# K's bias as a row added on VectorE, n3 made on ScalarE, and a new order of the opening, in a one-core transformer block

## The chip, the cores and the metric

The kernel runs on one core of a Trainium2 chip. The metric is the device time of one execution in microseconds (us). Below, PE is TensorE, DVE is VectorE, ACT is ScalarE, POOL is GpSimd and SP is SyncE, whose queue issues DMAs.

## The reference

There are 16 sequences of 256 tokens with 128 features, all in float32. Cut to what matters:

```python
sa, ca, ga, sb, cb, gb = modulation(silu(c) @ wmod)        # per sequence, gates clipped away from 0
h = layernorm(x) * (1 + ca) + sa
# attention layer with 16 heads of 8, softmax-free
Q = elu(h @ Wq + bq) + 1
K = elu(h @ Wk + bk) + 1
V = h @ Wv + bv
KV, Ksum = einsum(K, V), K.sum(tokens)
att = Q @ KV / (Q @ Ksum + 1e-6)                           # per head
x1 = layernorm(h + att @ Wo + bo) * g1 + beta1
z  = x1 + relu(x1 @ W1 + b1) @ W2 + b2                     # hidden width 512
x  = x + ga * (layernorm(z) * g2 + beta2)                  # x2 in the kernel
h2 = layernorm(x) * (1 + cb) + sb                          # n3 is this layernorm
xr, xk = token mixes of h2 and h2 one token before
out = x + gb * sigmoid(xr @ W_r) * (relu(xk @ W_k) ** 2 @ W_v)
```

## The kernel before, in words

Each engine runs a program that is written out by hand, and engines meet through semaphores alone: `need(engine, signal, count)` is a wait in front of the next instruction of that engine. An engine never passes a waiting instruction. A sequence is two chunks of 128 tokens (NC = 2).

The work is a pipeline over sequences. Step t starts sequence t (n1, K, Q, the state), and at the same time does the attention of sequence t-1, the feed-forward part of t-2, the second residual x2 and the norm n3 of t-3, and the mixing layer of t-4. Steps 0 to 2 are written out as `first_steps`. Steps 3 to 15 have a fixed order on each engine, and from step 4 on all parts are present, so that there are 12 full steps, 4 to 15. Step 16 drains, and a hand-written end finishes the last sequences.

What matters for one full step t, with the names used later:

- PE, in `step`: transposes of n1 (t), the attention product, transposes of ny (t-2), transposes of n3 (t-4), `k_product` (a bias product of line 1203 and four records of line 1206), `q_product`, three of four hidden products, attention transposes, the last hidden product, `state_product` (line 1222, it needs `k_ok`), `output_product`, then `mix_products`: line 1190, the key product of t-4, needs `mixk_ok`, the K half of the tile mixT, and line 1194, the receptance product, needs `mix_ok`, the R half. The feed-forward products of line 1140 end the step and raise `z_mm`.
- DVE, in `step`: it begins with `step_end`, whose statistics of z wait for `z_mm` of the step before. Then come the product with the tanh, the mean and variance of z, statistics of the next x, denominators and reciprocals, `centred`, `attention`, `k_elu`, `middle` (x2), the statistics of x2, and the two instructions of `mix_half`, K first. Later come the statistics of y, `q_elu`, the two instructions of `take_n3`, which wait for POOL's rstd of n3, `masked_state` and `y_norm`.
- ACT: hT and x1T out of the transposes, keepT, the exponents for K and Q, the hidden layer's relu, the state, and at the step's end tanh and n1 of the next sequence.
- POOL: each norm's power -0.5, and sums that need no PSUM.

K's bias in the kernel before is a product in bf16: the bias row is split into bf16 parts (`bias_part`), which stand in three rows of `bias_parts`, and each `k_product` multiplies them with `ones3` into bank 4 before the product with hT is added. exp_k and k_elu both read bank 4.

The first n1 is made from rstd and a shift: POOL multiplies mean and rstd (`mean_r`), subtracts (`shift_n1`), and then ACT takes chunk 0 and DVE chunk 1.

## Time and profile before

| what | value |
|---|---|
| median of 3 runs | 163.57 us (163.56 to 163.71) |
| the profiled execution | 162.83 us, its span 161.0 us |
| PE busy | 156.1 us, 97% of the span, granted clock full in all 40 slices |
| DVE busy | 128.8 us, 80% |
| ACT busy | 116.9 us, 73% |
| POOL busy | 105.1 us, 65% |
| chain that ended last | PE 88%, DVE 5%, POOL 2%, issue 2%, ACT 1% |

The span is the time on the core from the first to the last instruction. Busy time counts an engine's own instructions. In the chain each moment is given to the instruction for which the last one, followed back, had to wait.

### The profile page before, as it was taken

The page shows a single profiled execution, that of the slowest core. Times are in us where ns is not written, and L with a number is a line of the kernel's source. Part 1 is how long each engine was busy: PE and PEld are TensorE (multiplying, and loading weights), DVE is VectorE, ACT ScalarE, POOL GpSimd, SP SyncE. Part 2 cuts the span into 40 slices and gives each one's busy share as a digit, 9 for nine tenths or more (in the row PEclk, how much of TensorE's full clock was granted, in tenths as well). Part 3 has the DMA queues.
Part 4 walks back from the last instruction along what each step waited for, and adds up shares of the span by engine and source line. Part 5 has one row for each costly group of instructions (what it writes and reads, how often), then busy time and mean ns, then how long its engine had stood idle before and what let it go on. Part 6 is the DMA issues. An engine that isn't in the chain of part 4 may idle for free.

```text
span 161.0 us, 4072 instructions
## 1 busy us (share of the span) xinstructions
PE 156.1 (97%) x1151; PEld 145.8 (91%) x1151; DVE 128.8 (80%) x585; ACT 116.9 (73%) x320; POOL 105.1 (65%) x243
## 2 busy tenths in 40 slices
PE   7999999999999999999999999999999999999992
PEld 6878898999999999999999999999999999898891
DVE  3866878698888979797988888897979878887842
ACT  4256776789695969696987959595969787556562
POOL 4337567476676767787676767676777755972631
PEclk9999999999999999999999999999999999999999
DMA  4925279940010101010100101010101000010112
GB/s 124 255 100 160 80 215 338 429 199 0 2 33 4 33 0 33 4 35 2 33 5 0 33 6 33 0 33 4 33 2 35 4 4 28 2 37 2 33 29 69
DMA packets 8973, 9.93 MB, mean 62 GB/s; under 512 B 724, under 2 KB 7416, under 8 KB 8952
## 3 DMA queue, kind: packets, MB, share of 16 engines
q1 hardware_dynamic: 8656, 9.60, 19.1%
q8 instruction: 9, 0.15, 0.4%
q10 hardware_dynamic: 296, 0.08, 0.2%
q14 instruction: 12, 0.10, 0.2%
HBM read 7.55 MB, written 2.13 MB: 60 GB/s over the span
## 4 chain that ended last, share of the span: by engine, by line
PE 88%; DVE 5%; issue 2%; POOL 2%; ACT 1%; DVEq 0%; POOLq 0%
PE bank L1140 16%; PE bank L1250 15%; PE bank L1129 8%; PE bank L1222 5%; PE bank L1206 4%; PE bank L1178 4%; PE bank L1214 4%; PE bank L1166 4%; PE bank L1134 4%; PE bank L1362 3%; PE bank L1194 3%; PE bank L1190 3%; PE bank L1233 3%; PE bank L1070 2%; PE bank L1203 1%
## 5 line engine op out<-in xcount | busy, mean ns | idle before, releaser
L1140 PE MATMUL bank<-w,hid 128*128 128x128 f32 x240 | 31.7, 275 | 0.0
L1250 PE MATMUL bank<-x1T,w 128*128 128x256 f32 x120 | 30.9, 381 | 0.0
L1140 PEld LDWEIGHTS bank<-w,hid 128*128 128x128 f32 x240 | 29.3, 192 | 0.0
L347 ACT ACTIVATE hid<-bank,b_cols 128x256 f32<-128x256 f32 x60 | 26.0, 511 | 1.1 <-PE bank L1250 1.1
L534 POOL TENSOR_TENSOR rstd_n<-vare_n,power 128x2 f32<-128x2 f32 x30 | 23.8, 792 | 2.4
L323 ACT ACTIVATE hT<-bank,modT 128x256 f32<-128x256 f32 x16 | 9.0, 564 | 20.8 <-PE bank L1129 20.7
L1250 PEld LDWEIGHTS bank<-x1T,w 128*128 128x128 f32 x120 | 21.5, 190 | 2.6 <-ACT x1T L328 0.2
L530 POOL TENSOR_TENSOR vare_n<-mv_n,eps 128x2 f32<-128x2 f32 x30 | 5.8, 194 | 17.3 <-DVE mv_n L694 17.2
L292 ACT ACTIVATE n<-x_all,shift_n,rstd_n 128x128 f32<-128x128 f32 x27 | 11.8, 485 | 2.5 <-POOL shift_n L542 2.5
L700 DVE TENSOR_SCALAR ny<-bank,mv_ny,rstd_ny 128x128 f32<-128x128 f32 x32 | 11.6, 405 | 2.5 <-POOL rstd_ny L534 1.2
L700 DVE TENSOR_SCALAR n<-x,mv_n,rstd_n 128x128 f32<-128x128 f32 x28 | 8.4, 343 | 6.0 <-POOL rstd_n L534 6.0
L317 ACT ACTIVATE keepT<-bank,modT 128x255 f32<-128x255 f32 x26 | 13.1, 555 | 0.0
L534 POOL TENSOR_TENSOR rstd_ny<-vare_ny,power 128x2 f32<-128x2 f32 x16 | 11.9, 746 | 1.3
L588 POOL TENSOR_TENSOR out_sb<-x,prod 128x256 f32<-128x256 f32 x15 | 10.9, 726 | 2.8 <-DVE x L797 1.2
L685 DVE BATCH_NORM_STATS2 stats_z<-bank 128x6 f32<-128x128 f32 x30 | 7.4, 289 | 6.0 <-PE bank L1140 5.9
L1129 PE MATMUL bank<-ident,n 128*128 128x128 f32 x62 | 11.9, 273 | 0.0
L530 POOL TENSOR_TENSOR vare_z<-mv_z,eps 128x2 f32<-128x2 f32 x14 | 2.7, 195 | 13.7 <-DVE mv_z L694 13.7
L1166 PE MATMUL bank<-kqvo,attT 128*128 128x128 f32 x64 | 11.5, 275 | 0.0
L581 POOL TENSOR_TENSOR xb<-x_all,gm_rows 128x256 f32<-128x256 f32 x15 | 10.9, 724 | 0.8 <-DVE x L797 0.8
L822 DVE SCALAR_TENSOR_TENSOR mixT<-bank,modT,keepT 128x256 f32<-128x256 f32 x26 | 11.2, 470 | 0.0
L328 ACT ACTIVATE x1T<-bank,beta_b,cols 128x256 f32<-128x256 f32 x15 | 8.5, 563 | 3.7 <-PE bank L1129 2.5
L1178 PE MATMUL bank<-kvs,qT 128*128 128x144 f32 x64 | 10.7, 289 | 0.0
(186 smaller groups left out, 454.1 us busy)
## 6 DMA issues: line engine op xcount, KB each, us to landing
gm_rows<-mod_rows_dram SPq DMA_DIRECT2D x2, 960.0 KB, 9.6
out<-out_sb SPq DMA_DIRECT2D x15, 128.0 KB, 1.8
gm_rows<-mod_rows_dram SPq DMA_DIRECT2D x1, 768.0 KB, 6.8
w<-in_w SPq DMA_DIRECT2D x1, 512.0 KB, 5.5
x_all<-in_x SPq DMA_DIRECT2D x1, 512.0 KB, 5.5
bv_row<-bv_rows_dram SPq DMA_DIRECT2D x1, 512.0 KB, 7.7
bv_row<-bv_rows_dram SPq DMA_DIRECT2D x1, 384.0 KB, 4.3
gm_rows<-mod_rows_dram SPq DMA_DIRECT2D x1, 384.0 KB, 4.1
```

The source lines that it names most:

```text
L292: last = nc.scalar.activation(n1[s % 2][:, c, :], x_all[:, NC * s + c, :], ACT.Identity, scale=rstd["n1"][:, c:c + 1], bias=shift_n1[:, c: ...
L317: nc.scalar.activation(keepT[:, i, 1:L], banks[2][:, 0:L - 1], ACT.Identity, scale=mod_col(KEEP + i, s), bias=mod_col(SB, s)).then_inc((ke ...
L347: last = nc.scalar.activation(hid[:, f, :], bank[:, f % 2 * L:(f % 2 + 1) * L], ACT.Relu, bias=b1_cols[:, f:f + 1])
L534: nc.gpsimd.tensor_tensor(rstd[name][:, :], vare[name][:, :], power[:, :], ALU.pow).then_inc(rstd_ok[name], 1)
L581: nc.gpsimd.tensor_tensor(tile[:, :, :], x_all[:, NC * s:NC * (s + 1), :], gm_rows[:, s, GB_ROW:GB_ROW + 1, :].broadcast_to([128, NC, D]), ...
L700: last = nc.vector.tensor_scalar(dest[:, c, :], source(c), mv[name][:, c, 0:1], rstd[name][:, c:c + 1], ALU.subtract, ALU.mult)
L822: nc.vector.scalar_tensor_tensor(mixT[:, i, :], banks[2][:, 0:L], modT[:, MOVE + i, s:s + 1], keepT[:, i, :], ALU.mult, ALU.add).then_inc( ...
L1129: last = nc.tensor.transpose(bank[:, c * 128:(c + 1) * 128], tile[:, c, :], ident[:, :])
L1140: last = nc.tensor.matmul(banks[6][:, c * D:(c + 1) * D], hid[:, f, c * 128:(c + 1) * 128], w2[:, f, :], start=False, stop=(f == FF - 1 an ...
L1166: last = nc.tensor.matmul(banks[1][:, c * D:(c + 1) * D], attT[:, c * 128:(c + 1) * 128], wo, start=False, stop=(c == NC - 1))
L1178: last = nc.tensor.matmul(attention_bank(s)[:, c * (D + H):(c + 1) * (D + H)], qT[:, c * 128:(c + 1) * 128], kvs[:, :], start=True, stop=True)
L1250: return nc.tensor.matmul(bank[:, f % 2 * L:(f % 2 + 1) * L], w1[:, f * 128:(f + 1) * 128], x1T[:, :], start=True, stop=True)
```

## The change

Three things are changed together.

1. K's bias. Only sequence 0 still gets it by a product, now one float32 product of `ones_row` and `bias_rows`. For the others `k_product` has no bias product. DVE adds the bias row to bank 4 in a new instruction, `k_biased`, which writes kb, and exp_k and k_elu read kb. The casts and splits of `bias_part` are gone, and bk is loaded into 128 partitions instead of 3.
2. n3 in steps 3 to 15. The two instructions of `take_n3` leave DVE. DVE makes a small shift (`shift_of_n3`), and ACT makes n3 after n1 at its step's end. `centred` and the statistics of the next x change places in DVE's step.
3. The opening. The first n1 is made by DVE alone, both chunks, from mean and rstd as in the other norms, into the tile n1[1], and it is transposed from there. ACT makes n1[0] for the state product besides. Two warming products are gone, and `direct_row`, `direct_weights` and others come later.

```diff
             def k_exponent(s):
-                need(act, k_mm, s + 1)
-                nc.scalar.activation(exp_k[:, :, :], chunked(banks[4]), ACT.Exp, bias=neg1[:, :]).then_inc(expk_ok, 1)
+                if s == 0:
+                    act.wait_ge(k_mm, 1)
+                need(act, kb_ok, s)
+                source = kb[:, :, :] if s else chunked(banks[4])
+                nc.scalar.activation(exp_k[:, :, :], source, ACT.Exp, bias=neg1[:, :]).then_inc(expk_ok, 1)
...
+                if live(t):
+                    take_n3(t - 3)
+            def take_n3(s):
+                need(act, shift_ok, s + 1)
+                need(act, h2T_mm, s)
+                for c in range(NC):
+                    last = nc.scalar.activation(n3[:, c, :], x2[s % 3][:, c, :], ACT.Identity, scale=rstd["n3"][:, c:c + 1],
+                                                bias=shift_n3[:, c:c + 1])
+                last.then_inc(n3_ok, 1)
...
-            bias_part(0)
-            n1_chunk(0, 1).then_inc(n1_half, 1)
+            normalise("n1", n1[1], x_chunk(0), 1, n1_turn)
...
+            def shift_of_n3(s):
+                need(dve, rstd_ok["n3"], s + 1)
+                need(dve, n3_ok, min(s, LAST - 2))
+                nc.vector.scalar_tensor_tensor(shift_n3[:, :], mv["n3"][:, :, 0], -1.0, rstd["n3"][:, :], ALU.mult,
+                                               ALU.mult).then_inc(shift_ok, 1)
...
+            def k_biased(s):
+                need(dve, k_mm, s + 1)
+                need(dve, bias_rows_ok, 1)
+                nc.vector.tensor_tensor(kb[:, :, :], chunked(banks[4]), bias_rows[:, :].unsqueeze(1).broadcast_to([128, NC, D]),
+                                        ALU.add).then_inc(kb_ok, 1)
...
             def k_product(s):
+                if s == 0:
+                    pe.wait_ge(const_dve, 6)
+                    pe.wait_ge(bias_rows_ok, 1)
+                    nc.tensor.matmul(chunked(banks[4]), ones_row[:, :], bias_rows[:, :].unsqueeze(1).broadcast_to([128, NC, D]),
+                                     start=True, stop=False)
...
-                nc.tensor.matmul(chunked(banks[4]), ones3[:, :], bias_parts[:, :].unsqueeze(1).broadcast_to([128, NC, D]),
-                                 start=True, stop=False)
```

In a full step of DVE, from the mean and variance of z to the mixing, this stands in the kernel before (z is the centred z1, att the attention, x_2 the second residual, mixT the two mixing halves):

```order
L694 BN_AGGR mv_z<-stats_z 128x2 x2
L685 BN_STATS stats_n<-x_all 128x6 x2
L841 TENSOR_SCALAR den<-bank 128x32
L694 BN_AGGR mv_n<-stats_n 128x2 x2
L845 RECIPROCAL rden<-den 128x32
L787 SCALAR_TENSOR_TENSOR z<-bank,mv_z,gm_rows 128x128 x2
L850 TENSOR_TENSOR att<-bank,rden 128x128 x2
L836 SCALAR_TENSOR_TENSOR k_sb<-exp_k,bank 128x256
L797 SCALAR_TENSOR_TENSOR x_2<-z,rstd_z,xb 128x128 x2
L685 BN_STATS stats_n<-x_2 128x6 x2
L822 SCALAR_TENSOR_TENSOR mixT<-bank,modT,keepT 128x256 x2
```

The same stretch of DVE's step in the changed kernel:

```order
L711 BN_AGGR mv_z<-stats_z 128x2 x2
L796 SCALAR_TENSOR_TENSOR z<-bank,mv_z,gm_rows 128x128 x2
L856 TENSOR_SCALAR den<-bank 128x32
L860 RECIPROCAL rden<-den 128x32
L851 TENSOR_TENSOR kb<-bank,bias_rows 128x256
L865 TENSOR_TENSOR att<-bank,rden 128x128 x2
L702 BN_STATS stats_n<-x_all 128x6 x2
L711 BN_AGGR mv_n<-stats_n 128x2 x2
L846 SCALAR_TENSOR_TENSOR k_sb<-exp_k,kb 128x256
L806 SCALAR_TENSOR_TENSOR x_0<-z,rstd_z,xb 128x128 x2
L702 BN_STATS stats_n<-x_0 128x6 x2
L831 SCALAR_TENSOR_TENSOR mixT<-bank,modT,keepT 128x256 x2
```

The centred z moved to the front, the statistics of the next x behind the attention, and kb stands in front of the attention as a new instruction. All that stood ahead of mixT still does.

At the end of ACT's step and the start of the next one, the kernel before has:

```order
L433 ACTIVATE tanh_r<-bank 128x256
L292 ACTIVATE n_0<-x_all,shift_n,rstd_n 128x128 x2
L323 ACTIVATE hT<-bank,modT 128x256
L328 ACTIVATE x1T<-bank,beta_b,cols 128x256
L314 ACTIVATE keepT<-modT 128x2
```

and the changed kernel:

```order
L441 ACTIVATE tanh_r<-bank 128x256
L284 ACTIVATE n_0<-x_all,shift_n,rstd_n 128x128 x2
L451 ACTIVATE n<-x_2,shift_n,rstd_n 128x128 x2
L324 ACTIVATE hT<-bank,modT 128x256
L329 ACTIVATE x1T<-bank,beta_b,cols 128x256
```

The two instructions that make n3 stand between n1 and the hT of the next step.

## Rows read from the trace of the kernel before

**Rows 1.** Engines' busy us in 70 to 80 us: PE, PEld, DVE, ACT, POOL, clock, DMA

```profile
70.00:80.00 10.00, 10.00 (x75) 9.47 (x74) 8.66 (x40) 8.36 (x25) 7.54 (x17) 1.00 0.06 16
```

**Rows 2.** Timeline of PE in step 8: start us, length us, instruction

```profile
68.57 0.27 PE L1203 MATMUL bank<-bias_parts,ones 128*128 128x256 bf16 x1
68.68 0.61 PE L1206 MATMUL bank<-kqvo,hT 128*128 128x128 f32 x4
...
71.51 0.61 PE L1222 MATMUL bank<-k_sb,n 128*128 128x128 f32 x4
...
72.62 0.60 PE L1190 MATMUL bank<-mixT,mix_w 128*128 128x256 f32 x2
```

**Rows 3.** Timeline of DVE in the same step

```profile
67.62 0.49 DVE L685 BATCH_NORM_STATS2 stats_z<-bank 128x6 f32<-128x128 f32 x2 [0.44 <-PE bank L1140]
68.04 0.40 DVE L817 SCALAR_TENSOR_TENSOR prod<-tanh_r,bank 128x256 f32<-128x256 f32 x1
68.36 0.24 DVE L694 BATCH_NORM_AGGREGATE mv_z<-stats_z 128x2 f32<-128x6 f32 x2
68.52 0.45 DVE L685 BATCH_NORM_STATS2 stats_n<-x_all 128x6 f32<-128x128 f32 x2
69.00 0.19 DVE L841 TENSOR_SCALAR den<-bank 128x32 f32<-128x32 f32 x1
69.11 0.24 DVE L694 BATCH_NORM_AGGREGATE mv_n<-stats_n 128x2 f32<-128x6 f32 x2
69.27 0.32 DVE L845 RECIPROCAL rden<-den 128x32 f32<-128x32 f32 x1
69.50 0.51 DVE L787 SCALAR_TENSOR_TENSOR z<-bank,mv_z,gm_rows 128x128 f32<-128x128 f32 x2
69.93 0.48 DVE L850 TENSOR_TENSOR att<-bank,rden 128x128 f32<-128x128 f32 x2
70.52 0.42 DVE L836 SCALAR_TENSOR_TENSOR k_sb<-exp_k,bank 128x256 f32<-128x256 f32 x1
70.86 0.61 DVE L797 SCALAR_TENSOR_TENSOR x<-z,rstd_z,xb 128x128 f32<-128x128 f32 x2
71.50 0.49 DVE L685 BATCH_NORM_STATS2 stats_n<-x 128x6 f32<-128x128 f32 x2
...
76.40 0.50 DVE L685 BATCH_NORM_STATS2 stats_z<-bank 128x6 f32<-128x128 f32 x2 [0.44 <-PE bank L1140]
```

**Rows 4.** The first of the two mixing halves alone, the K half

```profile
71.90 0.47 DVE L822 SCALAR_TENSOR_TENSOR mixT<-bank,modT,keepT 128x256 f32<-128x256 f32 x1
```

**Rows 5.** Timeline, opening: a product of PE that had waited for DVE

```profile
9.14 0.42 DVE L836 SCALAR_TENSOR_TENSOR k_sb<-exp_k,bank 128x256 f32<-128x256 f32 x1 [0.64 <-ACT exp_k L333]
...
9.61 0.52 PEld L1222 LDWEIGHTS bank<-k_sb,n 128*128 128x128 f32 x4 [0.32 <-DVE k_sb L836]
9.61 0.71 PE L1222 MATMUL bank<-k_sb,n 128*128 128x128 f32 x4
```

**Rows 6.** Timeline of DVE in step 8, n3 and the masked state

```profile
74.30 0.60 DVE L700 TENSOR_SCALAR n<-x,mv_n,rstd_n 128x128 f32<-128x128 f32 x2 [0.50 <-POOL rstd_n L534]
74.82 0.30 DVE L858 TENSOR_TENSOR kvs<-bank,mask 128x144 f32<-128x144 f32 x1
```

**Rows 7.** Timeline of ACT in step 8 and the start of step 9

```profile
70.01 0.47 ACT L333 ACTIVATE exp_k<-bank,neg 128x256 f32<-128x256 f32 x1
...
74.29 0.87 ACT L292 ACTIVATE n<-x_all,shift_n,rstd_n 128x128 f32<-128x128 f32 x2
...
76.68 0.56 ACT L323 ACTIVATE hT<-bank,modT 128x256 f32<-128x256 f32 x1 [1.52 <-PE bank L1129]
```

**Rows 8.** Timeline, opening: POOL's part of the first n1, and ny of sequence 0

```profile
5.52 0.20 POOL L539 TENSOR_TENSOR mean_r<-mv_n,rstd_n 128x2 f32<-128x2 f32 x1
...
5.80 0.19 POOL L542 TENSOR_TENSOR shift_n<-one_pair,mean_r 128x2 f32<-128x2 f32 x1
...
18.95 0.44 PE L1129 MATMUL bank<-ident,ny 128*128 128x128 f32 x2
```

More of the change, by code:

```diff
@@ L76, in build @@
         bv_rows = sb("bv_rows", [S, D])
-        bias3 = sb("bias3", [3, D])
-        bias_k = sb("bias_k", [3, D])
-        part_mask = sb("part_mask", [3, 2])
-        high = [sb(f"high{i}", [3, D], BF16) for i in range(2)]
-        rest = sb("rest", [3, D])
-        bias_parts = sb("bias_parts", [128, D], BF16)
+        bk_rows, bias_rows = sb("bk_rows", [128, D]), sb("bias_rows", [128, D])
         x_all = sb("x_all", [128, S * NC, D])
@@ L88, in build @@
         hT = [sb(f"hT{p}", [128, L]) for p in range(2)]
+        kb = sb("kb", [128, NC, D])
         exp_k = sb("exp_k", [128, NC, D])
@@ L285, in _, with n1_part, take_n1 @@
             act.dma_start(bv_pad[0:1, :], a["bv"].rearrange("(a d) -> a d", a=1)).then_inc(bv_loaded, 16)
-            def take_n1(s, chunks=range(NC)):
+            def n1_part(s, c):
+                return nc.scalar.activation(n1[s % 2][:, c, :], x_all[:, NC * s + c, :], ACT.Identity,
+                                            scale=rstd["n1"][:, c:c + 1], bias=shift_n1[:, c:c + 1])
+            def take_n1(s):
                 need(act, aks_mm, s - 1)
@@ L290, in take_n1 @@
                 wait_x(act, s)
-                for c in chunks:
-                    last = nc.scalar.activation(n1[s % 2][:, c, :], x_all[:, NC * s + c, :], ACT.Identity,
-                                                scale=rstd["n1"][:, c:c + 1], bias=shift_n1[:, c:c + 1])
+                for c in range(NC):
+                    last = n1_part(s, c)
                 last.then_inc(n1_ok, 1)
-            take_n1(0, (0,))
+            act.wait_ge(x_in[0], 16)
+            act.wait_ge(shift_n1_ok, 1)
+            n1_part(0, 0)
             act.wait_ge(cols_ok, 2)
@@ L360, in first_steps @@
             def first_steps():
-                h_turned(0)
+                act.wait_ge(hT_mm, 1)
+                nc.scalar.activation(hT[0][:, :], banks[0][:, 0:L], ACT.Identity, scale=mod_col(CA, 0),
+                                     bias=shift_first[:, :]).then_inc(hT_ok, 1)
+                n1_part(0, 1).then_inc(n1_ok, 1)
                 k_exponent(0)
@@ L435, in step @@
                     take_n1(t + 1)
+                if live(t):
[3 more added lines that the diff above has]
+                need(act, h2T_mm, s)
+                for c in range(NC):
+                    last = nc.scalar.activation(n3[:, c, :], x2[s % 3][:, c, :], ACT.Identity, scale=rstd["n3"][:, c:c + 1],
+                                                bias=shift_n3[:, c:c + 1])
+                last.then_inc(n3_ok, 1)
             steps(step)
@@ L835, in k_elu @@
                 need(dve, expk_ok, s + 1)
-                nc.vector.scalar_tensor_tensor(k_sb[:, :, :], exp_k[:, :, :], 1.0, chunked(banks[4]), ALU.min,
-                                               ALU.max).then_inc(k_ok, 1)
+                plain = kb[:, :, :] if s else chunked(banks[4])
+                nc.vector.scalar_tensor_tensor(k_sb[:, :, :], exp_k[:, :, :], 1.0, plain, ALU.min, ALU.max).then_inc(k_ok, 1)
+            def k_biased(s):
[3 more added lines that the diff above has]
+                                        ALU.add).then_inc(kb_ok, 1)
             def denominators(s):
@@ L891, in first_steps @@
                 reciprocals(0)
+                k_biased(1)
                 attention(0)
+                direct_weights(1)
                 k_elu(1)
@@ L904, in first_steps @@
                 attention(1)
+                k_biased(2)
                 y_norm(0)
@@ L943, in step @@
                     mix_half(R_W, sc)
-                centred(sp_)
-                if not draining(t):
-                    attention(sb_)
-                if live(t):
+                    centred(sp_)
+                else:
                     k_elu(sa)
@@ L967, in step @@
                     gated(sc)
-                take_n3(t)
                 if live(t):
                     masked_state(sa)
+                    shift_of_n3(sp_)
+                else:
+                    take_n3(t)
                 if not y_first:
@@ L1044, in _ @@
             centred_last(0)
[L1045 to L1047 removed]
+            shift_of_n3(s14)
             z_norm_of_last(1)
```

108 lines of the change are left out of this document (47 added, 61 removed).

## The prediction

> **What bounds the kernel now.** I read the stretches table first: in 70 to 80 us PE is busy 10.00 of 10.00 us, while DVE has 8.66, ACT 8.36 and POOL 7.54 [rows 1]. So PE sets the pace of the full steps, at the full granted clock. The step's length is read off the statistics of z, which start at 67.62 and again at 76.40: 8.78 us [rows 3]. There are twelve full steps, 4 to 15, or 105 us of the 161. The next question is how near the other engines are to making PE wait. DVE waits 0.44 us for PE in front of the statistics of z, once per step [rows 3], and 0.50 us for POOL in front of n3 [rows 6]. These two look like room. But they lie at the ends of DVE's step, and what PE needs out of its middle must be read in order of time.
>
> PE needs the K half of mixT in front of line 1190. That product starts at 72.62 [rows 2]. The K half starts at 71.90 and takes 0.47, so it is there at 72.37 [rows 4]. What a product needs beyond the end of what it waits for is seen in the opening: the K tile ends at 9.14 + 0.42 = 9.56, the weights load at 9.61, and the four records take 0.71 instead of the 0.61 that they take in the gapless row [rows 2, 5]. I read this as 0.05 for the release and 0.10 for the load that is no longer hidden, 0.15 together. So the K half could be 72.62 - 0.15 - 72.37 = 0.10 us later than now and no more. That is the tight place of the step.
>
> **The change part by part.**
>
> *The bias product goes from PE.* Line 1203 starts at 68.57 and line 1206 at 68.68 [rows 2]: 0.11 us of PE's time per step. If nothing else came in the way, this would be 0.11 x 12 = 1.3 us in the full steps and 0.11 in step 3.
>
> *DVE's chain to the mixing.* I add up the gaps between starts, from the statistics of z to mixT. Before [rows 3, 4]: 0.42 to prod, 0.32 to mv_z, 0.16 to the statistics of x, 0.48 to den, 0.11 to mv_n, 0.16 to rden, 0.23 to z, 0.43 to att, 0.59 to k_sb, 0.34 to x, 0.64 to its statistics, 0.40 to mixT. The sum is 4.28, and the K half is ready at 4.75.
>
> In the changed order everything that stood ahead of mixT still does, and kb comes on top. 0.42 and 0.32 stay. z now follows mv_z at once and must wait for its end: 0.24 + 0.03 = 0.27 (the 0.03 is as between the end of x and its statistics, 71.47 to 71.50). z to den 0.43, as z to att now. den to rden 0.19 + 0.04 = 0.23, with nothing between them any more. rden to kb 0.23. kb to att: the trace has no such instruction; its length I bound by the masked state, 128x144 out of PSUM, 0.30 [rows 6], and by k_sb, 128x256 out of PSUM, 0.42, with the next start after 0.34 [rows 3]. The size is that of k_sb, so I take 0.34, with 0.22 (the shorter row less the same 0.08 of overlap) and 0.42 (no overlap) as ends. att to the statistics of x: today 0.59 passes to k_sb, but k_sb then waits for exp_k, which ends at 70.48 [rows 7]; without that wait a pair of 0.48 lets the next start some 0.09 before its end, as the pair z does, so 0.39. Statistics to mv_n 0.45 + 0.03 = 0.48. mv_n to k_sb 0.16. Then 0.34, 0.64 and 0.40 as now. The sum is 4.65, so mixT starts 0.37 us later after the statistics of z, and the K half is ready at 5.12.
>
> For PE, line 1190 then starts at 5.12 + 0.15 = 5.27 after the statistics of z. Today it is 72.62 - 67.62 = 5.00, and without the bias product it would be 4.89. So PE waits 0.38 us there in each full step. From line 1190 to the next statistics of z there are 76.40 - 72.62 = 3.78 us of PE's own work, which the change leaves as it is. The new step is 5.27 + 3.78 = 9.05 us against 8.78, or +0.27. This is a closed loop: z_mm lets DVE begin, DVE lets PE mix, PE makes the next z_mm. That DVE is idle afterwards doesn't help it. Twelve steps give +3.2 us.
>
> One rule of the Trainium skill bears on the unknown instruction. The trace says 0.34 us from k_sb, which reads PSUM, to the next start [rows 3]. The page "VectorE: DVE Perf Modes", section "The TRN2 errata", has 58 cycles plus the elements for a source in SBUF and 120 plus the elements for PSUM, at 0.96 GHz. By this, an estimate, kb costs 0.39 and k_sb out of kb 0.33, which makes the loop 0.04 longer per step, and the total 0.5 us more. I keep the trace's 0.34 for both.
>
> *n3 leaves DVE for ACT.* DVE loses 0.60 and its 0.50 of waiting [rows 6], both behind mixT, where DVE has room: nothing is gained. ACT gains 0.87, the price of the same kind of pair for n1 [rows 7]. It comes in front of hT, where ACT now waits 1.52 for PE [rows 7], so it is covered, with 0.65 left. Queued behind n3 on ACT is hT of the next step, and behind that K's product.
>
> *exp_k behind kb.* kb would start at 0.42 + 0.32 + 0.27 + 0.43 + 0.23 + 0.23 = 1.90 and end at 2.32. ACT comes to exp_k at 70.01 - 67.62 = 2.39 [rows 7]. So it costs nothing by 0.07. k_sb starts at 3.27 and ends at 3.69; the state product stands at 71.51 - 67.62 - 0.11 = 3.78 and could start at 3.84. That is 0.06 late, and inside the wait of line 1190 that follows.
>
> *The opening.* The first n1 no longer needs mean_r at 5.52 and the shift at 5.80 on POOL, which ends at 5.99 [rows 8]. So up to 0.5 us are won at 6 us. On the way to step 3 other things come in: k_biased for sequence 2 stands in front of the norm ny of sequence 0 on DVE, at 0.34, and PE takes ny's transposes at 18.95 as soon as they come [rows 8]. exp_k for sequences 1 and 2 waits for kb as well. I take -0.1 for the whole opening, with -0.6 and +0.3 as ends. Step 3 has no mixing, so there the 0.11 of the bias product is won in full.
>
> *The sum.* +3.2 in the full steps, -0.1 for step 3, -0.1 for the opening, and nothing for the end, whose order is unchanged: +3.0. The profiled execution took 162.83 around its span of 161.0, which gives 165.8; it lies 0.74 below the median of 163.57, on which I put the same difference: 166.6 us. With kb between 0.22 and 0.42, and 0.04 either way on the gaps that I joined, the loop grows by 0.25 to 0.49 before PE's 0.11 and the 0.10 of room are taken off, which is +0.15 to +0.39 per step and +1.8 to +4.7 in all. With the opening's ends the forecast's own range is 165.0 to 168.3.
>
> **The rivals.**
>
> *PE stays gapless.* Then the 0.11 is won in all steps from 1 on, 15 x 0.11 = 1.7, and with 0.1 of the opening the time is 161.8. This is the other side: it decides if the K half is ready by 4.89 - 0.15 = 4.74 after the statistics of z, that is if kb is paid for by what leaves the stretch. For it speaks that DVE sits idle 0.94 per step [rows 3, 6], that a wait of some 0.2 in front of k_sb goes, and that n3 leaves. Against it: the idle and n3 are behind mixT, the 0.2 is already in the sum above, and the room of 0.10 is smaller than any price of kb. Between this and the forecast lies a half-hidden loop, +0.0 to +0.1 per step, 163.4 to 165.0.
>
> *ACT becomes the bound.* n3 waits for DVE's shift, which waits for POOL's rstd, now later by the 0.37 of the mixing: about 74.3 + 0.37 + 0.2 = 74.9. ACT's n1 ends at 75.16, or 75.4 with PE's wait, so n3 ends near 76.3, and hT is wanted at 76.68 + 0.27. It decides from about 0.6 us more on ACT. If each step lost half a microsecond more, the time would be near 172; I see nothing in the rows that adds so much.
>
> *The change doesn't do what it says in the opening.* If kb and the new order eat more than the 0.5, the end is +0.3, which is within the forecast's range.
>
> **How the numbers follow.** The forecast has 0.76. PE gapless has 0.15, the half-hidden loop 0.06, and ACT as the bound 0.03. The forecast's own range holds about 0.70. To hold 8 in 10 I take in the half-hidden loop and a little beyond on both sides: 163.0 to 168.5. Faster by over 0.2%, about 0.3 us, which is what a measurement here tells from no change, is the gapless case and the best of the half-hidden one: 0.16. Within 0.2% is 0.03, slower 0.81.
>
> **What the changed profile would show.** If I am right, PE waits for DVE's mixT in front of the key product in each full step, 0.3 to 0.5 us, and nowhere else by as much. The statistics of z come every 9.05 us. From their start to mixT there are 4.65 us, with kb 0.42 long in between, and PE's busy share in 70 to 80 us falls to about 9.6. I would be wrong if PE stays at 10.00 with steps of 8.67, if mixT starts less than 4.4 us after the statistics of z, or if the wait stands at the state product or at hT instead.

## The result, and the profile after

| | before | changed |
|---|---|---|
| median of 4, us | 163.56 (162.94 to 163.71) | 169.06 (168.97 to 169.97) |
| profiled execution, us | 162.83 | 168.98 |
| its span, us | 161.0 | 167.3 |
| length of a full step, us | 8.78 | 9.28 |
| statistics of z of step 3 start at, us | 24.87 | 25.37 |

The ratio is 1.0356, with an interval of 1.0312 to 1.0401: 5.5 us slower. The forecast was 3.0 us slower, with a range up to 168.5 us, so the measured time lies 0.6 us above the range. The two profiled executions are 6.15 us apart, since that of the kernel before lay under the median it is compared with. In the later runs the kernel before has medians of 162.8 to 163.2 us, so 6 us is the better figure for the loss. Here and below a ratio leaves out executions over 1.5% above the fastest of their kernel, while medians and ranges have them all.

The stretches of the changed kernel (busy us of PE, PEld, DVE, ACT, POOL, then clock and DMA), which answer to [rows 1]:

```profile
60.00:70.00 10.00, 9.85 (x75) 9.04 (x74) 8.09 (x36) 8.61 (x24) 7.13 (x16) 1.00 0.05 15
70.00:80.00 10.00, 9.74 (x73) 8.84 (x72) 7.90 (x36) 8.16 (x22) 6.56 (x15) 1.00 0.05 15
```

PE is no longer at 10.00, and DVE and POOL are less busy too (8.66 and 7.54 before), as in a loop that waits for itself; ACT, which now makes n3, stands at 8.61 and 8.16 against 8.36. The row understates PE's wait. A step loses 0.57 us of 9.28 against the gapless 8.71 seen below, but the stretches show only 0.15 to 0.26 in ten, not the 0.4 that was forecast for this row: records of pipelined products overlap and cover gaps. DVE's step 7, from the statistics of z to the next ones, answers to [rows 3, 4]:

```profile
61.03 0.49 DVE L702 BATCH_NORM_STATS2 stats_z<-bank 128x6 f32<-128x128 f32 x2 [0.51 <-PE bank L1155]
61.44 0.41 DVE L826 SCALAR_TENSOR_TENSOR prod<-tanh_r,bank 128x256 f32<-128x256 f32 x1
61.76 0.24 DVE L711 BATCH_NORM_AGGREGATE mv_z<-stats_z 128x2 f32<-128x6 f32 x2
62.04 0.61 DVE L796 SCALAR_TENSOR_TENSOR z<-bank,mv_z,gm_rows 128x128 f32<-128x128 f32 x2
62.56 0.18 DVE L856 TENSOR_SCALAR den<-bank 128x32 f32<-128x32 f32 x1
62.78 0.35 DVE L860 RECIPROCAL rden<-den 128x32 f32<-128x32 f32 x1
63.05 0.36 DVE L851 TENSOR_TENSOR kb<-bank,bias_rows 128x256 f32<-128x256 f32 x1
63.33 0.48 DVE L865 TENSOR_TENSOR att<-bank,rden 128x128 f32<-128x128 f32 x2
63.72 0.48 DVE L702 BATCH_NORM_STATS2 stats_n<-x_all 128x6 f32<-128x128 f32 x2
64.33 0.25 DVE L711 BATCH_NORM_AGGREGATE mv_n<-stats_n 128x2 f32<-128x6 f32 x2
64.49 0.39 DVE L846 SCALAR_TENSOR_TENSOR k_sb<-exp_k,kb 128x256 f32<-128x256 f32 x1
64.80 0.61 DVE L806 SCALAR_TENSOR_TENSOR x<-z,rstd_z,xb 128x128 f32<-128x128 f32 x2
65.45 0.49 DVE L702 BATCH_NORM_STATS2 stats_n<-x 128x6 f32<-128x128 f32 x2
65.85 0.86 DVE L831 SCALAR_TENSOR_TENSOR mixT<-bank,modT,keepT 128x256 f32<-128x256 f32 x2
...
70.31 0.30 DVE L702 BATCH_NORM_STATS2 stats_z<-bank 128x6 f32<-128x128 f32 x1 [0.51 <-PE bank L1155]
```

mixT starts 65.85 - 61.03 = 4.82 us after the statistics of z (4.28 before, 4.65 forecast), and the next statistics come at 70.31, 9.28 us after the last. PE at the same place, then ACT's n3 and the hT behind it:

```profile
66.04 0.28 PE L1181 MATMUL bank<-kqvo,attT 128*128 128x128 f32 x1
66.43 0.30 PEld L1205 LDWEIGHTS bank<-mixT,mix_w 128*128 128x128 f32 x2 [0.31 <-issue]
66.46 0.67 PE L1205 MATMUL bank<-mixT,mix_w 128*128 128x256 f32 x2
...
68.94 0.86 ACT L451 ACTIVATE n<-x,shift_n,rstd_n 128x128 f32<-128x128 f32 x2
70.59 0.56 ACT L324 ACTIVATE hT<-bank,modT 128x256 f32<-128x256 f32 x1 [0.78 <-PE bank L1144]
```

The last product of the attention starts at 66.04 and would let the next follow 0.11 later; the key product starts at 66.46, with a first record that is longer by 0.07 than a gapless one (0.38). So PE stands some 0.4 us in front of the key product, as forecast. ACT waits 0.78 for PE after n3, so n3 is covered.

The opening. First the kernel before: PE's first products of kqvo in the timeline, and two of the loads of the first 16 us in the view of the DMAs (KB, median us from issue to landing).

```profile
3.92 0.79 PE L1082 MATMUL bank<-cols,kqvo 128*128 128x128 f32 x2
```

```profile
kqvo<-in_kqvo SPq DMA_DIRECT2D x2, 128.0 KB, 2.9
...
bias<-in_bk ACTq DMA_DIRECT2D x1, 1.5 KB
```

The same of the changed kernel, with ACT at sequences 1 and 2 in the timeline:

```profile
4.90 0.49 PE L1098 MATMUL bank<-cols,kqvo 128*128 128x128 f32 x2 [0.87 <-DMA kqvo<-in_kqvo]
...
18.83 0.51 ACT L337 ACTIVATE exp_k<-kb,neg 128x256 f32<-128x256 f32 x1 [1.51 <-DVE kb L851]
19.60 0.37 ACT L312 ACTIVATE attT<-bank 128x256 f32<-128x256 f32 x1
```

```profile
kqvo<-in_kqvo SPq DMA_DIRECT2D x2, 128.0 KB, 3.5
...
bk_rows<-in_bk ACTq DMA_DIRECT2D x1, 64.0 KB, 3.7
```

kqvo comes 1 us later than before. I had priced only the computing side of that load (128 partitions instead of 3), not its transfer. And exp_k of sequence 2 waits for a kb that stands behind the attention of sequence 1 on DVE.

Where the 6.3 us of span went: 0.50 up to step 3, 0.07 in step 3, 5.91 in the twelve full steps, and -0.18 at the end. The twelve steps are not all alike. Step 4 grows by 0.60 (8.55 to 9.15), steps 5 to 14 by 5.25 together, 0.50 or 0.51 each but for step 8 with 0.69, and step 15 by 0.06 only (8.78 to 8.84). Step 15 has no next x, so the statistics and mv_n are missing in its chain.

### The profile page after: what moved, and what is told of

It reads as the page before. It is cut to its first block, busy times and chain, and to the rows that moved or that the text cites. A ratio compares the mean times of both kernels' runs of the same rounds, so it can differ in the third digit from the quotient of the medians.

```text
span 167.3 us, 4103 instructions
## 1 busy us (share of the span) xinstructions
PE 159.2 (95%) x1133; PEld 143.6 (86%) x1133; DVE 129.0 (77%) x582; ACT 129.3 (77%) x347; POOL 105.3 (63%) x243
## 4 chain that ended last, share of the span: by engine, by line
PE 46%; DVE 35%; issue 10%; POOL 2%; DMA 2%; ACT 2%; DVEq 1%; SPq 0%; POOLq 0%
PE bank L1155 14%; DVE stats_n L702 6%; DVE x L806 5%; PE bank L1205 5%; DVE z L796 4%; PE bank L1380 3%; PE bank L1209 3%; DVE mixT L831 3%; PE bank L1270 3%; DVE att L865 3%; DVE kb L851 3%; DVE stats_z L702 3%; PE bank L1149 2%; PE bank L1253 2%; DMA kqvo<-in_kqvo 2%
## 5 line engine op out<-in xcount | busy, mean ns | idle before, releaser
L351 ACT ACTIVATE hid<-bank,b_cols 128x256 f32<-128x256 f32 x60 | 25.3, 489 | 1.2 <-PE bank L1270 1.2
L548 POOL TENSOR_TENSOR vare_n<-mv_n,eps 128x2 f32<-128x2 f32 x30 | 6.9, 230 | 22.5 <-DVE mv_n L711 22.3
L324 ACT ACTIVATE hT<-bank,modT 128x256 f32<-128x256 f32 x15 | 8.5, 565 | 11.0 <-PE bank L1144 11.0
L284 ACT ACTIVATE n<-x_all,shift_n,rstd_n 128x128 f32<-128x128 f32 x28 | 12.3, 486 | 2.6 <-POOL shift_n L560 2.6
L1242 PEld LDWEIGHTS bank<-k_sb,n 128*128 128x128 f32 x64 | 8.5, 190 | 4.6 <-DVE k_sb L846 4.5
L552 POOL TENSOR_TENSOR rstd_ny<-vare_ny,power 128x2 f32<-128x2 f32 x16 | 11.1, 691 | 1.2
L451 ACT ACTIVATE n<-x,shift_n,rstd_n 128x128 f32<-128x128 f32 x26 | 11.3, 482 | 0.2 <-DVE shift_n L788 0.2
L1242 PE MATMUL bank<-k_sb,n 128*128 128x128 f32 x64 | 11.1, 297 | 0.3
```

The source lines that it names most:

```text
L284: return nc.scalar.activation(n1[s % 2][:, c, :], x_all[:, NC * s + c, :], ACT.Identity, scale=rstd["n1"][:, c:c + 1], bias=shift_n1[:, c: ...
L351: last = nc.scalar.activation(hid[:, f, :], bank[:, f % 2 * L:(f % 2 + 1) * L], ACT.Relu, bias=b1_cols[:, f:f + 1])
L552: nc.gpsimd.tensor_tensor(rstd[name][:, :], vare[name][:, :], power[:, :], ALU.pow).then_inc(rstd_ok[name], 1)
L1242: last = nc.tensor.matmul(banks[3][:, 0:D], n1[s % 2][:, c, :], k_sb[:, c, :], start=(c == 0), stop=(c == NC - 1))
```

## The experiments

Each run is compared with the kernel before on the same chip. The kernel before took 162.84 us (162.73 to 163.52) beside the runs on the statistics, x2, the bias row and n3, 163.15 (162.71 to 164.58) beside those on the old order, the wide load, the late load and all edits, and 162.96 (162.61 to 163.91) beside the others.

### 1. What stands in DVE's chain

**The statistics of the next x at the tail of DVE's step** (changed kernel).

```diff
-                if live(t + 1):
-                    x_stats(t + 1)
-                    need(dve, mean_ok, sa + 1)
-                    norm_mv("n1", sa + 2)
...
+                if live(t + 2):
+                    x_stats(t + 2)
+                    x_mv(t + 2)
                 if live(t):
                     masked_state(sa)
```

> The changed kernel with one move on VectorE: the statistics and the mean and variance of the next x leave their place behind the attention and stand at the end of the step before, where VectorE waits for GpSimd. Loop theory (the statistics of z, VectorE's chain to the K half of mixT, the key product, the rest of TensorE's step): in the changed kernel mixT starts 4.82 us after the statistics of z and the step is 9.28. Without this pair k_sb is bound by exp_k only and starts at 2.97 instead of 3.46, so mixT starts at about 4.33, as in step 15 of the changed kernel (4.38, step 8.84), where the pair is missing anyway. The step becomes 8.8 and the time 169.06 - 11 x 0.46 = 164.0 us. Rival, ScalarE sets the pace since it also makes n3: the pair is not on ScalarE, the step stays at 9.28 and the time near 169.

Measured: 165.12 us (163.91 to 166.55), ratio 1.0103 [1.0051, 1.0155], steps of 8.84. Four of the 6 us are back by moving work that nobody waits for. The expected 164.0 is met by the profiled execution (163.91), while the median lies 1.1 us above it; the others are not profiled, so where they lose it isn't known. mixT starts 64.01 - 59.67 = 4.34 after the statistics of z. Of the 0.48 that this is earlier, the step gives back 0.44, because PE now finds the next wait:

```profile
59.67 0.49 DVE L702 BATCH_NORM_STATS2 stats_z<-bank 128x6 f32<-128x128 f32 x2 [0.51 <-PE bank L1156]
...
64.01 0.86 DVE L831 SCALAR_TENSOR_TENSOR mixT<-bank,modT,keepT 128x256 f32<-128x256 f32 x2
...
63.57 0.39 ACT L312 ACTIVATE attT<-bank 128x256 f32<-128x256 f32 x1
...
64.01 0.33 PE L1150 MATMUL bank<-ident,hT 128*128 128x128 f32 x1
...
64.73 0.60 PE L1206 MATMUL bank<-mixT,mix_w 128*128 128x256 f32 x2
```

attT ends at 63.96 and the output product, whose first record is the one with ident and hT, starts at 64.01, with a record of 0.33 instead of 0.27; the K half is there at 64.48, but PE comes to the key product only at 64.73.

**x2 in front of k_sb besides.**

```diff
-                else:
-                    k_elu(sa)
                 middle(sp_)
+                if not draining(t):
+                    k_elu(sa)
```

> As e1_stats_tail, and x2 (the instruction pair x<-z,rstd_z,xb) stands in front of k_elu instead of behind it, so that VectorE makes x2 while exp_k runs. Loop theory: mixT starts at about 3.9 to 4.0 us after the statistics of z, the K half is ready before TensorE asks for it, and TensorE has no wait there: the step is TensorE's own 8.67 and the time about 162.3 us. Rival, another wait of TensorE takes the place (the state product for k_sb, or hT of the next step, which stands behind n3 on ScalarE): the step stays at 8.75 or more and the time is 163.3 or more.

Measured: 164.59 us (164.05 to 165.43), ratio 1.01 [1.0052, 1.0149], steps still of 8.84. mixT is at 73.60 - 69.65 = 3.95 as expected, and it brings nothing: attT comes as late as before (74.00 for the output product, 4.35 after the statistics of z, against 4.34 above). The rival held in that another wait of PE takes the place, but it is the wait for attT, which the expectation did not name.

**No bias row** (changed kernel; it leaves K's bias out for all sequences but the first, so it computes something else and only its times are of use).

```diff
-                source = kb[:, :, :] if s else chunked(banks[4])
+                source = chunked(banks[4])
...
-                if live(t):
-                    k_biased(sa)
```

> The changed kernel with K's bias left out for all sequences but the first: no k_biased, exp_k and k_elu read bank 4. All else stands in its order. Loop theory: the chain loses the 0.28 us between the starts of kb and of the attention, mixT starts at 4.54, the step is 9.00 and the time about 165.6. If the added instruction were the whole of the loss, the step would be 8.67 or 8.78 and the time 162.5; if ScalarE set the pace, the step would stay at 9.28.

Measured: 168.53 us (2 runs, 168.06 and 169.00), ratio 1.0337 [1.0282, 1.0392], steps of 9.13 (four of 9.26 to 9.45). Expected were 9.00 and 165.6 us. A third of the missing 2.9 us lies in the opening: step 3 starts at 26.31, 0.94 later than in the changed kernel. The rest is in the steps, and the rows say why they are longer than 9.00:

```profile
80.00 0.50 DVE L700 BATCH_NORM_STATS2 stats_z<-bank 128x6 f32<-128x128 f32 x2 [0.50 <-PE bank L1149]
...
81.75 0.35 DVE L858 RECIPROCAL rden<-den 128x32 f32<-128x32 f32 x1
82.14 0.49 DVE L863 TENSOR_TENSOR att<-bank,rden 128x128 f32<-128x128 f32 x2
...
84.67 0.86 DVE L829 SCALAR_TENSOR_TENSOR mixT<-bank,modT,keepT 128x256 f32<-128x256 f32 x2
```

From rden to att it is 0.39 now, against 0.27 + 0.28 with kb between them: the attention waits for the end of rden, which kb had hidden. Taking kb away gains 0.15, not its 0.28.

**kb in the old order** (changed kernel, DVE's order of the kernel before up to the attention).

```diff
-                if live(t):
-                    centred(sp_)
+                if live(t + 1):
+                    x_stats(t + 1)
                 denominators(sb_)
+                if live(t + 1):
+                    need(dve, mean_ok, sa + 1)
+                    norm_mv("n1", sa + 2)
                 reciprocals(sb_)
                 if live(t):
+                    centred(sp_)
                     k_biased(sa)
                 attention(sb_)
```

> The changed kernel with DVE's step in the order of the kernel before up to the attention: statistics of the next x, den, mv_n, rden, z, then kb, attention, k_sb. So kb is the only thing added to the old chain. It tells what kb costs from what the new order costs. Theory (the new order costs most, because z then waits for mv_z and kb or the attention for rden with nothing between them): the chain is 4.28 plus kb's 0.28 = 4.56, and the step 4.56 + 0.47 + 0.21 + 3.78 = 9.02 us, 12 x 0.26 = 3.1 us below the changed kernel's 169.1: 166.0. Rival (kb itself costs what is lost, 9.28 - 8.67): steps stay near 9.28 and the time at 169.

Measured: 168.51 us (168.26 to 169.94), ratio 1.0345 [1.0293, 1.0397], steps of 9.18. My theory of 9.02 and 166.0 us fell:

```profile
62.81 0.49 DVE L702 BATCH_NORM_STATS2 stats_z<-bank 128x6 f32<-128x128 f32 x2 [0.51 <-PE bank L1155]
...
65.11 0.41 DVE L851 TENSOR_TENSOR kb<-bank,bias_rows 128x256 f32<-128x256 f32 x1
65.44 0.48 DVE L865 TENSOR_TENSOR att<-bank,rden 128x128 f32<-128x128 f32 x2
66.11 0.43 DVE L846 SCALAR_TENSOR_TENSOR k_sb<-exp_k,kb 128x256 f32<-128x256 f32 x1 [0.18 <-ACT exp_k L337]
...
67.50 0.86 DVE L831 SCALAR_TENSOR_TENSOR mixT<-bank,modT,keepT 128x256 f32<-128x256 f32 x2
...
67.49 0.33 PE L1149 MATMUL bank<-ident,hT 128*128 128x128 f32 x1 [0.19 <-ACT attT L312]
```

kb costs 0.33 to the next start here, and being later it holds up exp_k, so that k_sb waits: mixT at 4.69. attT is late by the same and sets the step. With this there are four corners for the start of mixT after the statistics of z: 4.28 old order without kb, 4.67 new order without kb, 4.69 old order with kb, 4.82 both. Each alone costs 0.4, both together 0.54. Neither is the cause by itself; they hide each other's waits. The times of these runs say less than their steps, since step 3 starts at 26.72 in this one, 1.35 later than in the changed kernel.

**n3 back on DVE.**

```diff
-                if live(t):
-                    take_n3(t - 3)
...
+                take_n3(t)
                 if live(t):
                     masked_state(sa)
-                    shift_of_n3(sp_)
```

> The changed kernel with n3 made by VectorE again in all steps, in front of the masked state as in the kernel before, and ScalarE free of it. Loop theory: n3 stands behind mixT, where VectorE has room, so the step stays at 9.28 and the time within 0.5 us of 169.06. Rival, ScalarE is made the bound by n3: the step falls to 8.8 to 9.0 and the time to 163 to 166 us.

Measured: 169.77 us (169.15 to 170.16), ratio 1.0401 [1.0361, 1.044], steps of 9.28. The time is 0.2 us beyond the half microsecond that was allowed, but step 3 starts at 26.82, 1.45 later than in the changed kernel, and the steps are the same. In the loop the move of n3 is worth nothing either way, and the rival in which ACT becomes the bound falls.

### 2. The opening

**Only the wide load, in the kernel before.**

```diff
-        bias3 = sb("bias3", [3, D])
+        bias3 = sb("bias3", [128, D])
...
-broadcast_to([3, D])).then_inc(bias_loaded
+broadcast_to([128, D])).then_inc(bias_loaded
```

> The kernel before with one edit: bk is loaded into 128 partitions (64 KB) instead of 3 (1.5 KB). The bias product and all else stay. In every profile so far that has the wide load, PE's first product of kqvo starts 0.9 to 1.2 us later than in the kernel before (3.92 us), PE stands idle in front of it, and its records shrink from 0.42 to 0.28 us later: at 5.8 before, but only near 9 us in two of the experiments. Theory (the wide load delays kqvo's transfer, and the idle time puts off the faster clock): first kqvo product at 4.8 to 5.1 us, z's statistics of step 3 at 25.4 to 26.8 instead of 24.87, steps unchanged at 8.78, time 163.4 to 164.7. Rival (the load is harmless and the new order of the opening is what costs): 3.9 us, 24.9 us, and 162.8 us.

Measured: 164.89 us (162.95 to 166.21, 12 runs), ratio 1.0067 [1.0032, 1.0103], steps of 8.78. In the profiled execution the statistics of z of step 3 start at 26.70 instead of 24.87. PE's opening in it:

```profile
4.83 0.80 PE L1082 MATMUL bank<-cols,kqvo 128*128 128x128 f32 x2 [0.80 <-DMA kqvo<-in_kqvo]
...
9.81 0.39 PE L1206 MATMUL bank<-kqvo,hT 128*128 128x128 f32 x2
```

So the load of 64 KB alone makes kqvo 0.9 us late. It costs 1.1 us by the ratio and 1.7 us in the median of all twelve runs; the medians of the spans are 160.9 and 162.8. In the profiled execution step 3 is 1.8 us late, more than the delay of kqvo, and PE's records there stay at the slower clock until 9.8 us instead of 5.8, on which more is said at the end. The twelve spans fall in two groups, two of 161.2 and 161.5 and ten of 162.5 to 163.3. That the two had the faster clock early would fit, but they are not profiled.

**bk's load last on ACT's queue, bias_rows later** (changed kernel).

```diff
             act.dma_start(bv_pad[0:1, :], ...).then_inc(bv_loaded, 16)
+            act.dma_start(bk_rows[:, :], ...broadcast_to([128, D])).then_inc(bias_loaded, 16)
...
             nc.vector.tensor_tensor(shift_first[:, :], ...).then_inc(cols_ok, 1)
+            dve.wait_ge(bias_loaded, 16)
+            nc.vector.scalar_tensor_tensor(bias_rows[:, :], ...).then_inc(bias_rows_ok, 1)
```

> The changed kernel with bk's wide load issued last on ACT's queue, behind cols and bv, and with bias_rows computed after the shift of the first n1, so that it doesn't hold up what waits for cols. Theory of the wide load: kqvo's first product at about 3.9 us, the faster PE records before 6 us, z's statistics of step 3 at 24.6 to 25.2, steps 9.28 as in the changed kernel, and 168.0 to 168.6 us against its 169.1. Rival (kqvo is late for another reason, such as the queue's order): kqvo's product stays at 4.9 and the time at 169.1. Third: the late bias_rows hold up the f32 bias product of sequence 0 and the gain is lost.

Measured: 173.63 us (172.72 to 174.29), ratio 1.0638 [1.0593, 1.0683]. kqvo is on time, and yet it is the worst of all:

```profile
3.82 0.63 PE L1098 MATMUL bank<-cols,kqvo 128*128 128x128 f32 x2
...
9.88 0.94 PE L1218 MATMUL bank<-bias_rows,ones_row 128*128 128x256 f32 x2 [3.20 <-DVE bias_rows L748]
```

Issued at 3.6 us instead of 1.3, while x and wmod are being loaded, the load lands 5.8 us after its issue instead of 3.7, and the f32 bias product waits 3.20 us for it. The third case that was named came: step 3 starts at 29.10, and the run takes 4.6 us more than the changed kernel. Part of that is PE's clock: its records still have 0.42 us when the wait ends, and keep that length until 13.4 us; the granted clock is 0.53 in 10 to 12 us and 0.61 in 12 to 14.

**A narrow load for sequence 0, the wide one late** (changed kernel).

```diff
+            act.dma_start(bk3[:, :], ...broadcast_to([3, D])).then_inc(bk3_loaded, 16)
...
+            nc.vector.scalar_tensor_tensor(bias_first[0:3, :], bk3[:, :], 1.0, banks[6][0:3, D:2 * D], ALU.add,
+                                           ALU.subtract).then_inc(bias_first_ok, 1)
...
                 masked_state(0)
+                dve.wait_ge(bias_loaded, 16)
+                dve.wait_ge(bv_ok, 1)
+                nc.vector.scalar_tensor_tensor(bias_rows[:, :], bk_rows[:, :], 1.0, banks[6][:, D:2 * D], ALU.add,
+                                               ALU.subtract).then_inc(bias_rows_ok, 1)
```

> The changed kernel with that opening alone: bk for sequence 0 from the load into 3 partitions, the wide load late, the rows after the masked state. The loop is that of the changed kernel. Theory: kqvo at 3.8 to 3.9 us, steps 9.28, z's statistics of step 3 at 24.8 to 25.1 (the first n1 gains 0.5, kb(2) in front of exp_k costs up to 0.8), time 168.3 to 168.9 against 169.1 and with a smaller spread. Rival (the wide load cost the changed kernel nothing in the median): 169.1 to 169.5.

Measured: 168.51 us (168.30 to 168.63), ratio 1.0325 [1.0297, 1.0353], steps of 9.28, step 3 at 25.18. It is as expected, but for 0.1 in step 3. The median is 0.55 us under that of the changed kernel. The intervals of the two ratios overlap, but all five spans (166.6 to 166.9) lie under its four (167.2 to 168.2), so the wide load at its early place cost it about half a microsecond and most of its spread.

**Four more warming products** (changed kernel).

```diff
-            keep_warm(WARM)
+            keep_warm(WARM + 4)
```

> The changed kernel with 4 more warming products in front of kqvo's first product, 10 instead of 6, so that PE works on until kqvo comes (4.03 + 4 x 0.21 = 4.87 us; it waits until 4.9 now). Theory (the idle 0.9 us puts off the faster clock in some executions): PE's records go from 0.42 to 0.28 us before 6.5 us, step 3 at 25.2 to 25.5, time 168.5 to 169.1, and no execution over 169.4. Rival (the moment of the faster clock has nothing to do with the idle time): records stay at 0.42 us until 8 us or later in some, with times to 170, as now.

Measured: 170.06 us (169.27 to 170.76), ratio 1.0419 [1.038, 1.0459], step 3 at 25.69. I had counted 0.21 us for a product, but each is two records, 0.43, so the four held kqvo's product up to 5.33. The theory's time of 168.5 to 169.1 was missed. The profiled execution had the faster records by then; the others are not profiled, and the four spread over 1.5 us. It settles nothing on what moves the faster clock.

### 3. Toward a better version

**All edits, with bk last and attT taken before the first hidden piece.**

```diff
-                hidden_out(sd, 0)
                 attention_turned(sb_)
+                hidden_out(sd, 0)
```

> The changed kernel with all edits that the runs point to: the statistics of the next x at the tail of DVE's step, x2 in front of k_sb, and for sequence 2 kb in front of the attention; on ACT the attention's transposes are taken before the first hidden piece, in the steps and in the opening; bk's load last on ACT's queue. With the first two alone the step was 8.84, with PE waiting for attT. Theory (attT is the last wait that stood there, about 0.12 us, and hT's 0.05 stays): steps 8.72, and z's statistics of step 3 at 24.4 to 24.9, so 162.1 to 162.7 us, at or just under the kernel before. Rival (attT comes late because exp_k waits for kb, not because of its place on ACT): steps stay at 8.84, and the time is 163.4 to 164.

Measured: 167.23 us (166.74 to 167.84), ratio 1.0242 [1.0202, 1.0281]. The expected 162.1 to 162.7 us was missed in the opening, which has a wait of 4.2 us for bias_rows as in the other run with the late load, a granted clock of 0.50 behind it (in 10 to 14 us), and step 3 at 30.42. The steps are 8.71, as the theory of attT has it:

```profile
76.90 0.38 ACT L312 ACTIVATE attT<-bank 128x256 f32<-128x256 f32 x1
...
77.58 0.27 PE L1150 MATMUL bank<-ident,hT 128*128 128x128 f32 x1
...
78.24 0.60 PE L1206 MATMUL bank<-mixT,mix_w 128*128 128x256 f32 x2
```

attT is there 0.3 us early, the record is back at 0.27, and PE is gapless.

**The same with the narrow load** (bk3 and the late wide load, as in the run with the narrow load above).

> The changed kernel with the loop's edits of the last one (steps of 8.71 us there) and another opening: the f32 bias product of sequence 0 takes bk from a load into 3 partitions, issued where the kernel before has it, and the wide load for kb goes last on ACT's queue, its rows being made after the masked state of sequence 0, where DVE waited 0.46 us. The late wide load landed at 9.7 to 10.6 us; here nothing wants it before 11.5. Theory (the wide load cost the opening, the chain and attT the steps, and nothing else does): first kqvo product at 3.8 to 3.9 us, z's statistics of step 3 at 24.4 to 25.0, steps 8.71; with the 135.7 us from there to the end that the last one had, a span of 160.1 to 160.7 and 162.0 to 162.7 us. Rival (the opening has another loss): step 3 at 25.5 or later, and 163.5 us or more.

Measured: 162.26 us (162.15 to 162.56, 9 runs) against 162.96 of the kernel before, ratio 0.9952 [0.9932, 0.9971]. It beats both kernels, the one before by half a percent. Its steps are 8.71 and step 3 starts at 25.06. Its DVE:

```profile
67.90 0.50 DVE L706 BATCH_NORM_STATS2 stats_z<-bank 128x6 f32<-128x128 f32 x2 [0.73 <-PE bank L1164]
...
71.84 0.86 DVE L835 SCALAR_TENSOR_TENSOR mixT<-bank,modT,keepT 128x256 f32<-128x256 f32 x2
...
76.61 0.30 DVE L706 BATCH_NORM_STATS2 stats_z<-bank 128x6 f32<-128x128 f32 x1 [0.79 <-PE bank L1164]
```

and its stretch of 70 to 80 us, to be read against [rows 1]:

```profile
70.00:80.00 10.00, 10.00 (x74) 9.40 (x73) 8.76 (x41) 9.31 (x26) 7.33 (x17) 1.00 0.05 14
```

mixT starts 3.94 after the statistics of z, with kb in the chain. Step 3 is a little later than expected (24.4 to 25.0), though the first transposes start 0.5 us earlier than before (6.12 against 6.66). The traces show where the opening loses this again, 0.7 us up to step 3. The lead is gone at the masked state of sequence 1, which starts at 16.00 on DVE against 15.99 before; in front of it DVE waits 0.18 for ACT's relu of Q, which in ACT's new order stands behind attT and the exponent of Q and starts at 15.02 against 14.67. Then kb of sequence 2 stands in front of the attention, which starts at 17.94 against 17.77, and PE stays 0.17 to 0.19 behind from there to step 3.

**Two of the moves in the kernel before.**

```diff
+                middle(sp_)
                 if live(t):
                     k_elu(sa)
-                middle(sp_)
```

> The kernel before with two of the moves that helped the changed one: x2 in front of k_sb on DVE, and the attention's transposes taken in front of the first hidden piece on ACT. There PE is gapless in the steps, so taking time off DVE's chain should bring nothing. Theory: steps 8.78, 162.8 us. Rival (short waits hide in the gapless row): steps of 8.70 and 161.9 us.

Measured: 163.23 us (162.96 to 163.79), ratio 1.0007 [0.9983, 1.003], steps of 8.77. Where PE is gapless, a shorter chain brings nothing. So the 0.07 us per step of the best version are the bias product's. They are not its whole balance, though. In the profiled executions it wins 0.65 in steps 5 to 14, but loses 0.43 in steps 3, 4 and 15 and 0.19 in the opening, so that step 16 starts at the same time (137.81 against 137.84). The end is 0.21 shorter, and that is nearly all of the 0.24 by which the profiled span falls.

## Why the prediction was right and where it failed

**The mechanism was right.** PE waits for the K half in front of the key product in each full step, and behind it come 3.78 us of PE's own work: 66.46 + 0.07 to 70.31, as in [rows 2, 3]. PE gapless, the rival of the other side, fell with the first profile, and ACT as the bound with the run that puts n3 back.

**The step that failed is the sum of the chain in the loop, mis-sized with PE's release by 0.23 us per step.** 9.05 was forecast, 9.28 came.

| from, to (start to start) | forecast | measured |
|---|---|---|
| z, den | 0.43 | 0.52 |
| rden, kb | 0.23 | 0.27 |
| kb, att | 0.34 | 0.28 |
| statistics of x, mv_n | 0.48 | 0.61 |
| k_sb, x | 0.34 | 0.31 |
| the other eight | 2.83 | 2.83 |
| statistics of z to mixT | 4.65 | 4.82 |
| end of the K half to PE's effective start | 0.15 | 0.21 |

The one instruction that the trace did not show, kb, was priced well within its bounds, at 0.34 for 0.28. What failed was the step "I add up the gaps between starts" for the gaps that the new order joins. mv_n stands right behind its statistics now and starts 0.13 after their end, where I had put 0.03 from the pair of x and its statistics. The pair z takes 0.61 instead of 0.51, and its second one starts 0.26 after the first instead of 0.17; it does so in each of the versions in which z comes right after mv_z, and not in the run with the old order (0.51). Why the pair is longer I did not find out. I had allowed 0.04 for all joined gaps, and they made 0.26. PE's release took 0.21 instead of 0.15; the key product waits on two semaphores there, but no run tells this apart from others.

The larger of these gaps stood in the trace of the kernel before, outside of the full steps, at the places where the same two instructions are neighbours:

```profile
17.38 0.35 DVE L845 RECIPROCAL rden<-den 128x32 f32<-128x32 f32 x1
17.77 0.49 DVE L850 TENSOR_TENSOR att<-bank,rden 128x128 f32<-128x128 f32 x2
...
19.53 0.48 DVE L685 BATCH_NORM_STATS2 stats_n<-x_all 128x6 f32<-128x128 f32 x2
20.14 0.25 DVE L694 BATCH_NORM_AGGREGATE mv_n<-stats_n 128x2 f32<-128x6 f32 x2
```

mv_n starts 20.14 - 20.01 = 0.13 after the end of its statistics here too, and the attention starts 0.39 after rden, which is what the run without the bias row found. In all traces the gap between statistics and their mean and variance goes with the number of semaphore waits in front: 0.03 or 0.04 with one, 0.10 or 0.11 with two, 0.13 with three. No run varies that number alone, so this is not shown to be the cause.

The forecast took twelve equal steps, 0.27 x 12 = 3.2 us; they made 5.91. These 2.7 us are the most of the 3.3 that the forecast of +3.0 lacks against the 6.3 of the span. The sum of the range has two slips besides. With kb at 0.22 and 0.04 off the gaps the chain grows by 0.37 - 0.12 - 0.04 = 0.21, not 0.25; and only the 0.10 of room is taken off after that, not PE's 0.11, which the step doesn't gain while PE waits. Neither touches the upper end, and that is the end which was passed.

On the page "VectorE: DVE Perf Modes" of the Trainium skill, section "The TRN2 errata", kb would cost 0.39 and k_sb 0.33, by an estimate from its cycles. The rows have 0.28 and 0.31 to the next start, with lengths of 0.36 and 0.39; so the page's figures are within 0.03 and 0.06 of the lengths, but not what a chain pays. By them the step would be 9.09, nearer to the 9.28 measured, but for a reason that the rows don't bear out.

**The opening was mis-sized, by 0.6 us.** The forecast was -0.1 with ends of -0.6 and +0.3; it was +0.50. Two steps of it failed. I looked at what the bias load is for, not at the 64 KB that it adds to queues that carry kqvo: alone it costs the kernel before 1.1 us by the ratio and 1.7 in the median, and the changed one 0.55. The delay reaches the first n1 too. On DVE it stands behind bq_col, which waits for a product of kqvo and starts at 5.65 instead of 5.17. So n1 starts at 5.92, and the first transposes at 6.66, as in the kernel before, with nothing won; with the narrow load they are at 5.32 and 6.09. And the wait of exp_k of sequence 2 for kb was named, but not priced: 1.51 us on ACT, which makes attT of sequence 1 late. Putting kb in front and taking attT first brought step 3 from 25.18 to 25.06, so it was worth little. Smaller terms: step 3 was forecast at -0.1 and came at +0.07, and the end was put at nothing, as its order was said to be unchanged, and came at -0.18.

**The bias product was priced at 0.11, and is worth 0.07.** The gapless versions have 8.71 against 8.78. hT comes just too late once the product in front is gone: in the changed kernel the product of hT takes 0.66 instead of 0.61, and PE's stretch from n1's transposes to the query product is shorter by 0.06.

That it came out slower rests on the loop alone, and the rows of before held enough for it: the room of 0.10 us in front of the key product [rows 2, 4] against any price of kb.

## What to carry to other kernels

Where one engine is gapless, look for the last point at which it could wait and how much room is there; an instruction of 0.3 us in the chain to that point costs time in every turn, even if its engine is idle a tenth of the time. What it costs depends on its neighbours: kb lengthened the chain by 0.15 us in the new order and by 0.41 in the old. Work that nobody waits for goes behind that point: moving the statistics of the next x with their mean and variance brought back four of six microseconds. A gap between starts may be carried to a new order only if the same two instructions are neighbours in it. Look for such a pair anywhere in the trace, the opening and the drain included, before taking another pair's gap; the pairs that became neighbours here came out up to 0.13 us longer than put. And a small constant broadcast to 128 partitions is a transfer like any other: ask what lands at the same time.

## What the runs showed of the hardware

- The clock of PE in the opening. The clock column shows 1.00 from the start in all profiles, but the records don't: the 128-column f32 products are 0.42 us long and 0.21 apart, and later 0.28 and 0.11, which is 1.2 and 2.4 GHz. The faster records begin at 5.8 us in the kernel before, at 4.9 in the changed one, at 9.8 in the kernel before with the wide load, and between 8.8 and 10 in four of the experiments on the changed one. In these five late cases PE had stood idle for 0.64 to 1.04 us in front of kqvo, from about 4.0 on; but so it had, for 0.87 and 0.74, in the changed kernel and in one experiment, where the faster records came right behind the wait. Step 3 follows: 26.3 to 26.8 in the late ones, 25.3 to 25.4 in the early ones, 25.1 to 25.2 in the two with the narrow load and no idle time, where the faster records begin at 6.4 to 7.2. Their times spread over 0.3 to 0.4 us, against 0.9 to 3.3 with the idle time (the kernel before, which has none, over up to 1.9). What decides the moment stays open.
- The clock behind a long wait. In the two runs with the late load PE stood idle for 3.20 and 4.16 us in front of the bias product. In the second the records had been 0.28 us long from 5.2 us on, and behind the wait they were 0.42 long again until 15.2; the granted clock was 0.50 in 10 to 14 us, the lower of the two levels. In the first they had 0.42 all along before the wait, and shrank only at 13.4 us.
- The same load lands sooner or later by what is in line before it: bk's 64 KB took 3.5 to 3.9 us when issued at 1.3 us, and 5.7 to 6.5 when issued at 3.4 to 3.7, while the median time of kqvo's two loads went from 3.5 to 3.8 down to 2.4 to 2.9 (2.3 and 2.9 with a narrow load alone).
- exp from SBUF is 0.51 long, from PSUM 0.47, with the next start after 0.41 and 0.36.
